# Layer 1 attention of a four-layer conditioned transformer: rotary partner rows by exchange transfers instead of products with swapped weights

## The reference

```python
def _rope(x):
    cos, sin = ...                       # per token and frequency
    x0, x1 = x[..., 0::2], x[..., 1::2]
    o0 = x0 * cos - x1 * sin
    o1 = x1 * cos + x0 * sin
    return jnp.stack([o0, o1], axis=-1).reshape(x.shape)

qkv = x @ w_qkv + b_qkv                  # x: (64, 64, 256), normalised and modulated
q, k, v = jnp.split(qkv, 3, axis=-1)
q = _rope(q.reshape(B, T, 16, 16)); k = _rope(k.reshape(B, T, 16, 16))
attn = softmax(q @ k^T / 4); out = attn @ v; x = x + out @ w_ao + b_ao
```

## Time and profile before

| | us |
|---|---|
| median of three runs | 2149.86 |
| lowest and highest run | 2144.82, 2150.0 |
| the profiled execution | 2150.09 |
| its span in the profile | 2148.3 |

### The profile page before, as it was taken

How to read it: one execution, slowest core, us unless ns; L and a number is a source line. 1 busy time by engine, 2 the same in 40 slices (tenths; PEclk the granted TensorE clock), 3 DMA queues, 4 the chain that set the end, 5 groups by cost and what they waited for, 6 DMA issues and landing times.

```text
span 2148.3 us, 44435 instructions
## 1 busy us (share of the span) xinstructions
PE 2049.8 (95%) x15652; PEld 1670.8 (78%) x15652; DVE 1314.9 (61%) x2537; ACT 987.4 (46%) x1581; POOL 405.0 (19%) x381
## 2 busy tenths in 40 slices
PE   7999999999999999999999999998999999998998
PEld 6887887778777888877777777776888777787887
DVE  5856565767766565654444555456666677775664
ACT  3444555444444333334444444445444555454443
POOL 3632112223221010101111111112001222210000
PEclk9999999999999999999999999999999999999999
DMA  6000000000000000000000000000000000000000
GB/s 224 21 10 8 7 11 15 9 7 15 7 8 13 18 20 10 20 5 7 7 6 5 5 0 5 5 2 16 5 5 5 16 6 10 10 1 9 21 20 30
DMA packets 18405, 33.38 MB, mean 16 GB/s; under 512 B 1298, under 2 KB 12050, under 8 KB 17810
## 3 DMA queue, kind: packets, MB, share of 16 engines
q1 hardware_dynamic: 18322, 32.25, 4.7%
HBM read 28.06 MB, written 4.19 MB: 15 GB/s over the span
## 4 chain that ended last, share of the span: by engine, by line
PE 79%; DVE 9%; issue 7%; ACT 2%; POOL 2%; DMA 0%; DVEq 0%; SPq 0%; ACTq 0%; POOLq 0%
PE psum L591 21%; PE psum L593 20%; PE psum L592 19%; PE psum L688 4%; PE psum L701 3%; PE psum L633 2%; PE psum L720 2%; PE psum L786 2%; PE psum L734 2%; PE psum L677 1%; DVE xn L1093 1%; PE psum L526 1%; DVE h_lo L1114 1%; DVE pb L1169 1%; PE psum L685 1%
## 5 line engine op out<-in xcount | busy, mean ns | idle before, releaser
L591 PE MATMUL psum<-h_hi,w_lo 128*128 128x512 f32 x1120 | 463.4, 414 | 11.7 <-DVE h_lo L1114 6.3
L593 PE MATMUL psum<-h_hi,w_hi 128*128 128x512 f32 x1120 | 441.6, 394 | 0.0
L592 PE MATMUL psum<-h_lo,w_hi 128*128 128x512 f32 x1120 | 440.8, 394 | 0.0
L1221 DVE TENSOR_TENSOR hid_lo<-hid,hid_hi 128x512 fp32r<-128x512 f32 x256 | 194.0, 759 | 266.2 <-ACT hid_hi L967 265.9
L967 ACT ACTIVATE hid_hi<-hid 128x512 fp32r<-128x512 f32 x256 | 161.7, 632 | 223.1 <-PE psum L593 133.0
L591 PEld LDWEIGHTS psum<-h_hi,w_lo 128*128 128x128 f32 x1120 | 212.4, 190 | 62.4 <-issue 11.0
L593 PEld LDWEIGHTS psum<-h_hi,w_hi 128*128 128x128 f32 x1120 | 211.8, 189 | 49.5
L592 PEld LDWEIGHTS psum<-h_lo,w_hi 128*128 128x128 f32 x1120 | 212.6, 190 | 39.0
L1303 POOL TENSOR_TENSOR rstd<-ms,half_t 128x4 f32<-128x4 f32 x64 | 65.4, 1021 | 903.9 <-DVE ms L1088 485.1
L1166 DVE TENSOR_REDUCE mx<-psum 128x8 f32<-128x512 f32 x192 | 132.4, 690 | 160.0 <-PE psum L677 106.7
L962 ACT ACTIVATE hid<-psum,vec 128x512 f32<-128x512 f32 x192 | 131.8, 687 | 182.8 <-PE psum L593 166.9
(11 more groups left out here) (140 smaller groups left out, 3601.1 us busy)
## 6 DMA issues: line engine op xcount, KB each, us to landing
stage<-in_w_dram SPq DMA_DIRECT2D x24, 256.0 KB, 2.7
stage<-in_w_dram SPq DMA_DIRECT2D x8, 512.0 KB, 3.5
out_dram<-xres SPq DMA_DIRECT2D x8, 512.0 KB, 2.9
xres<-in_x_dram SPq DMA_DIRECT2D x1, 3584.0 KB, 18.4
modw_mod<-in_modw_dram SPq DMA_DIRECT2D x2, 1536.0 KB, 13.6
stage<-in_w_dram SPq DMA_DIRECT2D x8, 384.0 KB, 3.3
stage<-in_w_dram SPq DMA_DIRECT2D x8, 192.0 KB, 2.4
modw_film<-in_modw_dram SPq DMA_DIRECT2D x1, 1024.0 KB, 7.4
```

Source lines behind the costliest of these rows:

```text
L591: nc.tensor.matmul(dst, s_lo, m_hi, start=start and j == 0, stop=False)
L592: nc.tensor.matmul(dst, s_hi, m_lo, start=False, stop=False)
L593: ins = nc.tensor.matmul(dst, s_hi, m_hi, start=False, stop=stop and j == len(pairs) - 1)
L1221: nc.vector.tensor_tensor(hid_lo[:, slot, :], hid32[:, slot, :], hid_hi[:, slot, :].bitcast(F32), ALU.subtract).then_inc(sem["hid"], 1)
```

## The change

Partner rows are no longer computed by TensorE. ScalarE copies the rows of q or k with their bias from PSUM to `rows1`; SyncE copies even rows to odd and odd rows to even rows of `swapped`, by two transfers of 64 partitions; GpSimd multiplies `swapped` by the sine and adds it to `q32` or `k32`, where VectorE has put the rows times the cosine. In layer 1's attention ScalarE also does `norm` instead of VectorE. The list of stages of layer 1 is written anew, with the new stages `k_swap`, `q_swap` (SyncE) and `k_rot`, `q_rot` (GpSimd). SyncE now follows the list too; `load` is its stage for the weights. The tiles from `at_hi` on lie 64 bytes further. The swapped weights are still laid out and loaded, and not used.

```diff
+    if layer == 1:
+        return [own("scores", 0), prev("probs_t", 7), own("k", 1), prev("pv", 6), own("q", 1), own("k_swap", 1),
+                own("q_swap", 1), own("share"), nxt("load"),
+                own("scores", 1), own("probs_t", 0), own("v", 0), prev("pv", 7), own("v_out", 0), own("k_rot", 1), own("v", 1),
+                own("v_out", 1), nxt("stats"),
+                own("scores", 2), nxt("norm"), own("probs_t", 1), prev("merge"), own("k_out", 1), own("q_rot", 1), own("pv", 0),
+                own("scores", 3), own("probs_t", 2), prev("proj"), own("pv", 1), own("q_out", 1), nxt("turn"),
+                own("scores", 4), own("probs_t", 3), prev("back"), nxt("split"), own("pv", 2),
+                own("scores", 5), own("probs_t", 4), own("pv", 3), nxt("k", 0), nxt("q", 0), nxt("k_swap", 0),
+                nxt("q_swap", 0),
+                own("scores", 6), own("probs_t", 5), own("pv", 4), nxt("k_rot", 0), nxt("q_rot", 0),
+                own("scores", 7), own("pv", 5), own("probs_t", 6), nxt("k_out", 0), nxt("q_out", 0)]
...
-        at[0] += 32 - at[0] % 64
+        at[0] += (160 - at[0]) % 256
...
+                elif s in ("q_swap", "k_swap"):
+                    which, name = "qk".index(s[0]), s[0]
+                    added = f"{name}32"
+                    wait_alone(sp, sem[f"{name}_rows"], n_at(f"{name}_rows", ph, b, k + 1))
+                    wait_alone(sp, sem[added], n_at(added, ph, b, k))
+                    for odd in range(2):
+                        sp.dma_start(swapped[odd:P:2, which, :],
+                                     rows1[1 - odd:P:2, which, :]).then_inc(sem[f"{name}_swapped"], 16)
...
                     up_rows(ph, s, k, b, 0, (0 if s == "q" else width) + k * P)
-                    if layer == 1:
-                        up_rows(ph, s, k, b, 1, (768 if s == "q" else 1024) + k * P)
...
+                elif s == "norm" and PHASES[ph] == ("attn", 1):
+                    act.wait_ge(sem["rstd"], n_at("rstd", ph, b, 1))
+                    for t in range(TILES):
+                        ins = nc.scalar.activation(xn[:, t, :], xres[:, b * TILES + t, :], ACT.Copy, scale=rstd[:, t:t + 1])
+                    ins.then_inc(sem["normed"], 1)
+                elif s in ("q", "k") and layer == 1 and kind == "attn":
+                    which = "qk".index(s)
+                    bank, at = a_slot(ph, s, k, b)
+                    act.wait_ge(sem[f"a_full{bank}"], at + 1)
+                    act.wait_ge(sem[f"{s}_swapped"], n_at(f"{s}_swapped", ph, b, 32 * k))
+                    nc.scalar.activation(rows1[:, which, :], acc_a[bank], ACT.Identity,
+                                         bias=col(f"{s}1", k)).then_inc(sem[f"{s}_rows"], 1)
...
-                    for u, (bias, tab, cnt) in enumerate(((f"{s}1", "cos", "rot_a"), (f"{s}s1", "sin", "rot_b"))):
-                        bank, at = a_slot(ph, s, k, b, u)
...
+                    dve.wait_ge(sem[f"{s}_rows"], n_at(f"{s}_rows", ph, b, k + 1))
+                    dve.wait_ge(sem[s], n_at(s, ph, b, (2 if s == "q" else 4) * k))
+                    nc.vector.scalar_tensor_tensor(by_seq((q32 if s == "q" else k32)[:, :]), by_seq(acc_a[bank]), col(f"{s}1", k),
+                                                   col("cos", 0, S).unsqueeze(1).to_broadcast([P, SEQ, S]),
+                                                   ALU.add, ALU.mult).then_inc(sem[f"{s}_cos"], 1)
...
+                elif s in ("q_rot", "k_rot"):
+                    which, name = "qk".index(s[0]), s[0]
+                    pool.wait_ge(sem[f"{name}_swapped"], n_at(f"{name}_swapped", ph, b, 32 * (k + 1)))
+                    nc.gpsimd.tensor_tensor(by_seq(swapped[:, which, :]), by_seq(swapped[:, which, :]),
+                                            col("sin", 0, S).unsqueeze(1).to_broadcast([P, SEQ, S]),
+                                            ALU.mult).then_inc(sem[f"{name}_sin"], 1)
...
+                    nc.gpsimd.tensor_tensor(dst, dst, swapped[:, which, :], ALU.add).then_inc(sem[f"{name}32"], 1)
```

More of the change, by code:

```diff
@@ L92, in order_of @@
     if kind == "mlp":
-        return [own("up", 2), own("down", 0), nxt("stats"), prev("back"), own("share"), own("up", 3), nxt("norm"),
+        return [own("up", 2), own("down", 0), nxt("stats"), prev("back"), own("share"), nxt("load"), own("up", 3), nxt("norm"),
                 own("down", 1), own("up", 4), own("down", 2), own("up", 5), own("down", 3), nxt("turn"),
@@ L99, in order_of @@
                 nxt("turn"), prev("pv"), prev("back"), nxt("split"), own("scores"), own("v", 0), own("v", 1),
-                own("exp"), own("share"), own("bias")]
-    if layer in (1, 3):
-        mask = (lambda c, off: [("mask", c, off)]) if layer == 3 else (lambda c, off: [])
-        return mask(1, 0) + [own("scores", 0), prev("probs_t", 7), own("q", 1), own("q_out", 1), prev("pv", 6), own("share"),
+                own("exp"), own("share"), own("bias"), nxt("load")]
+    if layer == 1:
[10 more added lines that the diff above has]
+                own("scores", 7), own("pv", 5), own("probs_t", 6), nxt("k_out", 0), nxt("q_out", 0)]
+    if layer == 3:
+        return [own("mask", 1), own("scores", 0), prev("probs_t", 7), own("q", 1), own("q_out", 1), prev("pv", 6), own("share"), nxt("load"),
                 own("scores", 1), own("probs_t", 0), own("v", 0), prev("pv", 7), own("v_out", 0), own("v", 1),
@@ L109, in order_of @@
                 own("scores", 4), own("probs_t", 3), prev("back"), nxt("split"), own("pv", 2),
-                own("scores", 5)] + mask(0, 1) + [own("probs_t", 4), own("pv", 3), nxt("k", 0), nxt("k_out", 0),
+                own("scores", 5), nxt("mask", 0), own("probs_t", 4), own("pv", 3), nxt("k", 0), nxt("k_out", 0),
                 own("scores", 6), own("probs_t", 5), own("pv", 4), nxt("q", 0), nxt("q_out", 0),
@@ L115, in order_of @@
             own("divide", 0), own("scores", 1), prev("pv", 7), own("exp", 1), own("q", 2), own("k", 2), own("probs_t", 0),
-            own("v", 0), prev("proj", 7), own("share"), own("v", 1), own("v", 2), own("v", 3), prev("back"), own("v", 4),
+            own("v", 0), prev("proj", 7), own("share"), nxt("load"), own("v", 1), own("v", 2), own("v", 3), prev("back"), own("v", 4),
             own("v", 5), own("v", 6), own("v", 7)]
@@ L140, in fills_in @@
     if kind == "attn" and s in ("q", "k", "v"):
-        return 2 if layer == 1 and s != "v" else 1
+        return 1
     return 1 if kind == "attn" and layer == 2 and s == "probs_t" else 0
@@ L170, in counts_of @@
     if layer == 1:
-        c.update(rot_a=4, rot_b=4, k32=2)
+        c.update({f"{s}_{what}": 64 if what == "swapped" else 2 for s in "qk" for what in ("rows", "cos", "swapped", "sin")})
+        c.update(k32=2)
     if layer == 3:
@@ L287, in build @@
         on = place("on", [P, SEQ, P], F32, free + 8192 + 16384 + 8704)
-        rot = place("rot", [P, 2, 2, BLK], F32, rot_at)
-        assert free + 8192 + 16384 + 8704 + 4096 <= wb
+        q32 = place("q32", [P, BLK], F32, free + 8192 + 16384 + 8704 + 4096)
+        k32 = place("k32", [P, BLK], F32, gate_at)
+        rows1 = place("rows1", [P, 2, BLK], F32, rot_at)
+        swapped = place("swapped", [P, 2, BLK], F32, rot_at + 4096)
+        assert free + 8192 + 16384 + 8704 + 4096 + 2048 <= wb
         free3 = wa + 8 * 2048
@@ L397, in run_phases @@
                             stage_of(0, "table", TABLE_AFTER.index((s, k)), blocks - 1)
-                    elif coming and coming[0][0] == s and s in ("stats", "norm", "turn", "split"):
+                    elif (s, k) in coming and s in ("stats", "norm", "turn", "split", "load"):
                         stage_of(ph + 1, s, k, 0)
-                        coming = coming[1:]
+                        coming.remove((s, k))
             for s, k in stages(phases - 1, -1):
@@ L515, in _ @@
+            run_phases(stage_of, sp)
             sp.wait_ge(stored, 16 * blocks)
@@ L1088, in stage_of @@
                         nc.vector.tensor_scalar(ms[:, :], mv[:, :, 1], EPS[layer], None, ALU.add).then_inc(sem["rstd_in"], 1)
-                elif s == "norm":
+                elif s == "norm" and PHASES[ph] != ("attn", 1):
                     dve.wait_ge(sem["rstd"], n_at("rstd", ph, b, 1))
```

65 lines of the change are left out of this document (24 added, 41 removed).

## The result

The changed kernel takes 2192.6 us (median of four runs, 2191.4 to 2193.4); the kernel before, run beside it, 2149.3. The ratio is 1.0205, interval 1.0188 to 1.0223: slower by 43 us, where 28 was forecast. The profiled execution took 2191.4 us, its span is 2189.6.

What follows compares the result with a forecast made beforehand. TensorE, busy 95% of the span, was taken as the bound. The profiled 2150.1 + 10.5 (seven turns) + 2 (first block) + 16 (clock) = 2178.6, stated as 2178 us; range 2140 to 2200 us.

Steps and rivals of the forecast that it cites:

- likeliest case: Whole kernel: the prediction's own forecast, slower at 2178 us, with its own range of 2162 to 2190 us; chance 0.56.
- the three places: Layer 1's attention: 0.4 + 0.4 + 0.7 = +1.5 us a steady block, +10.5 over seven turns, +2 for the first block.
- What was taken away: Layer 1's attention: 24 partner-row products fewer on TensorE in a block, 5.5 us, 44 us over eight blocks.
- Place 1: Turn of the block: TensorE waits 4.7 us for pt, kx and qb where it waited 1.6; net +0.4 us.
- rival of late transfers: Layer 1's exchanges: they land in 3.5 us or more, not 2.3; +8 up to +20 us, 2186 to 2198; chance 0.15.
- Place 2: Merge to projection: ScalarE's norm waits for rstd ahead of pt and at_hi; TensorE waits 0.9 + 2.2 us, net +0.4.
- rival of a hidden wait: Merge to projection: rstd is there when ScalarE reaches norm, so no wait; 2147 us, or 2141; chance 0.20.
- Place 3: Projection to scores 4: qb stands behind y on ScalarE, TensorE waits 1.4 us, half counted as given back: +0.7.
- the 42 to 44 named as a sign: Layer 1's attention: blocks of 42 to 44 us would show the forecast right, blocks under 39.5 us wrong.
- The clock: After TensorE's waits in layer 1: 13.5 drops to the lower level instead of 4, 1.7 us each, +16 us.
- The rest: Buffers moved by 64 bytes: 0, with ends of -3 and +3 us; SP's loads in the new order: 0.
- Port contention: Layer 1's attention: GpSimd's new products stop VectorE where both work in SBUF; +9 us, 2187; chance 0.08.

Runs made afterwards that it cites:

- the three runs: Changed kernel without the exchange transfers: 2187.2 us; with k_out 0 and q_out 0 ahead of probs_t 6 instead: 2192.0 us; with both edits: 2159.3 us.

## Why the prediction was right, and where its size was off

Slower was forecast, by 28 us, and slower by 43 came. 2192.6 us is inside the outer range, but beyond the 2162 to 2190 that the prediction gave its likeliest case. The mechanism of the three places is the one that was forecast; the sizes of the clock, the addresses and layer 2 were not.

**What was taken away**: right. 192 products fewer, 5.5 us a block.

**Place 1**: right, and for the reason given. 4.7 us forecast, 4.95 measured; "transfers hidden but without slack" is what the three runs show, and in the changed kernel's trace the two branches end 0.06 us apart. The transfers took 2.0 us to landing in the median (2.3 taken), and GpSimd's product with a broadcast 1.27 us where 1.05 was taken; these nearly cancel. So the rival of late transfers is out: taking them away entirely gave 0.3 us a turn.

**Place 2**: right in form, two pieces, before probs_t 2 and before the projection. 0.9 + 2.2 = 3.1 was forecast, 1.38 + 2.02 = 3.40 came; the norm took 1.70 us, not 1.4. The rival of a hidden wait needed rstd 2 us earlier, and ScalarE stood 1.57 us for it. Moving the norm to VectorE gave 4.6 us in the stage where it stood ahead of at_lo, and 28.5 where it stood behind (some 20 by the medians): what stands behind it in the list counts.

**Place 3**: the mechanism is there, 1.14 us where 1.4 was worked out. The step that counted half of it as given back is the weak one: a wait of 1.14 us stood in full in the blocks, 0.4 more than the 0.7 counted, and the next wait for h (0.38 us) stood behind it. Together a steady block loses 2.3 us in waits less products, where +1.5 was forecast, and the whole block takes 44.5 us, just above the 42 to 44 named as a sign. In the last block, for which the prediction counted nothing, TensorE waited 3.01 us before its projection.

**The clock**: the direction is right, the sum too small. 13.5 drops of 1.7 us were forecast where 4 were before, +16 us. The trace has 16 stretches at the lower level in the stage against 4: in or behind all eight turns, all seven waits before a projection and one more wait of the first block. Three of them are twice as long as any before, and they are 51.2 us more in all. Subtracting waits and products leaves +20 us for it, and with the 3.6 us that the addresses gave back (the run with the new address alone) +24, where +16 stood. Half of 51.2 us, what half pace would cost a TensorE without pauses, is 25.6, an estimate near that. With the three places (+17.5, not +12.5) layer 1's attention comes to +37.8 instead of +28.5. These are the mis-sized terms of the stage.

**The rest**: this is the term that failed. "0, with ends of -3 and +3" for the 64 bytes was -12 us by the run with that line alone (ratio 0.9944), outside its bound: the row it rested on, 0.23 us for a product from either buffer, is rounded too coarsely to show 5 ns, and 5 ns over some thousands of products is the whole effect. And layer 2 was not in the sum at all: +12.3 us of stops for instructions. The two errors nearly cancelled (-8.8 outside both attentions), so the total looks better than its parts. So the total owes its nearness in part to luck. The prediction named this sign itself, blocks elsewhere that differ by more than 0.3 us; they do (0.3 us in each MLP block), and the addresses were the cause there.

**Port contention**: not met in the changed kernel, as argued, but it appeared at once when the norm went back to VectorE.

**Its working**: in the rival of the hidden merge wait, 2147 less seven times the 0.7 of place 3 is 2142, not 2141; nothing hangs on it.

## What to carry to other kernels

Products removed from a bound engine are worth only what does not stand as cover over another engine's chain; before removing them, lay the chain of each neighbouring engine beside the gap, and refill it with products whose inputs are ready. Here the norm on VectorE and late in the list turned +2.1% into +0.6%, and the list that lays the next block's k 1 and v 0 into the gap turned that into -1.1%; the new addresses, which give the kernel before 0.6% by themselves, are in all of these. Where two chains end within 0.1 us of each other, test edits together as well as one by one: each alone shows nothing. A total can agree by errors that cancel, so compare stage by stage, the untouched stages too.

## What the hardware showed that was not expected

- The place of some operands' buffers within 256 bytes changes TensorE's pace: 600 products of the first MLP in 128.79 us at one offset and 127.01 at the other, the same to 0.01 us in two different kernels, and 12 us over the whole kernel before.
- A loop body of some 1626 TensorE instructions is fetched again in some turns of the loop and not in others, as the packets in the traces have it: 2.5 + 2.0 us of standing still and a clock drop behind it, a turn of 71.2 or 70.3 us instead of 63.8, twice in one kernel, three times in another, never in a third.
- VectorE's `tensor_scalar` of 256 columns takes 348 ns alone (the median) and up to 1422 ns beside GpSimd's products; the more of it a GpSimd instruction overlaps, the longer it takes.
- An exchange of neighbouring partitions from SBUF to SBUF (two transfers, 128 KB each by the profile) took 2.0 us from issue to landing in the median of 64.
